# Scores and value products of a local attention in four parts a tile, and a new order of steps on four engines

## What is computed

```python
# per layer i, per batch b:       x: 256 tokens x 128 channels
q, k, v = split(shift_tokens(x) @ Wqkv[i])            # 16 heads of 64
q, k = rotary(l2norm(q) * qs), rotary(l2norm(k) * ks)
# windows of 32 queries, each sees its own 32 keys and the 32 before
sim  = einsum('bhwie,bhwje->bhwij', bq, bk2) * 8      # 32 x 64 scores
attn = softmax(where(mask, -max, sim), -1)
out  = einsum('bhwij,bhwje->bhwie', attn, bv2)        # 32 x 64 values
x = out @ Wo[i] + x
xn = layernorm(shift_tokens(x)) * g + bln
a, gate = split(xn @ W1[i] + b1, 2)
x = a * gelu(gate) @ W2[i] + b2 + x
```

## Time and profile before

| | us |
|---|---|
| median of 3 runs | 3975.99 (3974.95 to 3983.92) |
| the profiled execution | 3987.9 |
| its span, first to last instruction | 3986.1 |
| PE busy | 3633.8 (91%), 64569 matmuls |
| DVE busy | 2734.0 (69%) |
| ACT busy | 2766.0 (69%) |
| POOL busy | 1037.4 (26%) |

### The profile page before, as it was taken

The page is one execution under the profiler, slowest core; times in us unless marked ns, Lnnn a source line. Parts: engine busy times, 40 slices in busy tenths (PEclk is TensorE's granted clock), DMA queues, the critical chain, the costliest instruction groups (busy, mean ns, idle before and its releaser), DMA issues.

```text
span 3986.1 us, 157311 instructions
## 1 busy us (share of the span) xinstructions
PE 3633.8 (91%) x64569; PEld 2525.9 (63%) x64761; DVE 2734.0 (69%) x5376; ACT 2766.0 (69%) x9073; POOL 1037.4 (26%) x857
## 2 busy tenths in 40 slices
PE   6776999999999999999999999999999999999997
PEld 3333666666666666666666666666666666666665
DVE  3334777777777777777777777777777777777774
ACT  3443776776777776777777677777777777777775
POOL 0001232232232233232223223223223223223220
PEclk7556999999999999999999999999999999999998
DMA  1001555445455445455545454545554545544452
GB/s 49 7 7 31 115 115 121 108 106 137 105 119 122 107 111 136 107 121 117 116 111 125 114 125 105 124 106 123 122 117 109 120 112 123 115 114 110 111 121 68
DMA packets 361465, 421.61 MB, mean 106 GB/s; under 512 B 52480, under 2 KB 266000, under 8 KB 360000
## 3 DMA queue, kind: packets, MB, share of 16 engines
q1 hardware_dynamic: 360768, 411.67, 44.8%
HBM read 19.30 MB, written 2.10 MB: 5 GB/s over the span
## 4 chain that ended last, share of the span: by engine, by line
PE 77%; ACT 9%; issue 5%; DVE 0%; SPq 0%; DMA 0%; POOL 0%; DVEq 0%; ACTq 0%
PE ring_ps L1062 18%; PE out_ps L1176 8%; PE ring_ps L1109 7%; PE score_ps L1127 7%; PE out_ps L1204 7%; PE out_ps L1164 7%; ACT probs L659 6%; PE turn_ps L1146 6%; PE turn_ps L1138 4%; PE small_ps L1073 4%; PE turn_ps L1211 2%; PE score_ps L1117 2%; ACT att_t L647 1%; ACT L641 1%; PE out_ps L1194 1%
## 5 line engine op out<-in xcount | busy, mean ns | idle before, releaser
L659 ACT ACTIVATE probs<-score_ps,neg_max,rq 128x64 f32<-128x64 f32 x3072 | 1191.7, 418 | 185.9 <-DVE neg_max L876 184.7
L838 DVE TENSOR_TENSOR prod<-ring_ps,tables 128x512 f32<-128x512 f32 x1536 | 951.4, 681 | 157.3 <-PE ring_ps L1062 146.5
L532 POOL TENSOR_TENSOR ks<-prod 128x1024 f32<-128x1024 f32 x192 | 451.5, 2352 | 2102.8 <-DVE prod L838 2018.6
L1062 PE MATMUL ring_ps<-xs,wqk 128*128 128x256 f32 x3072 | 765.7, 387 | 11.9 <-DVE xs L825 5.1
L614 ACT ACTIVATE square<-ring_ps,biases 128x512 f32<-128x512 f32 x768 | 507.1, 687 | 252.0 <-DVE prod L838 229.7
L659 ACT ACTIVATION_READ_ACCUMULATOR probs<-score_ps,neg_max,rq 128x1 f32 x3072 | 673.6, 219 | 0.0
L1062 PEld LDWEIGHTS ring_ps<-xs,wqk 128*128 128x128 f32 x3072 | 555.5, 191 | 116.3 <-issue 41.1
L647 ACT ACTIVATE att_t<-turn_ps 128x512 f32<-128x512 f32 x384 | 229.3, 597 | 501.0 <-PE turn_ps L1146 501.0
L532 POOL TENSOR_TENSOR qs<-prod 128x1024 f32<-128x1024 f32 x192 | 451.9, 2354 | 243.5 <-DVE prod L838 235.9
L1164 PE MATMUL out_ps<-v,pt 64*32 64x64 f32 x24576 | 349.7, 224 | 88.5 <-issue 87.1
L1109 PE MATMUL ring_ps<-wv,xs 128*128 128x512 f32 x768 | 405.5, 631 | 1.0 <-issue 1.0
(11 more groups left out here) (156 smaller groups left out, 4483.7 us busy)
## 6 DMA issues: line engine op xcount, KB each, us to landing
v<-vs SPq DMA_DIRECT2D x1344, 128.0 KB
qt<-qs SPq DMA_DIRECT2D x768, 128.0 KB
kt<-ks SPq DMA_DIRECT2D x768, 128.0 KB
v<-vs SPq DMA_DIRECT2D x192, 64.0 KB
wqk<-in_L_ffn_Wqkv SPq DMA_DIRECT2D x6, 1024.0 KB, 5.2
wv<-in_L_ffn_Wqkv SPq DMA_DIRECT2D x6, 512.0 KB
wo<-in_L_ffn_Wo SPq DMA_DIRECT2D x6, 512.0 KB
prod<-in_L_attn_x SPq DMA_DIRECT2D x16, 128.0 KB, 2.1
```

The lines of the kernel that those rows point to most:

```text
L532: pool.tensor_tensor(dst, prod_a[p % 2], prod_b[p % 2], ALU.add).then_inc(rot_ready, 1)
L659: last = nc.scalar.activation(probs[i][:, j, e, :], score_ps[e][:, KEYS * j:KEYS * (j + 1)], ACT.Exp, bias=neg_max[:, h:h + 1], scale=rq[p ...
L838: last = V.tensor_tensor((prod_b if a else prod_a)[p % 2][:, f, :] .rearrange("p (u c) -> p u c", u=2), bank[:, :].rearrange("p (u c) -> p ...
L1062: last = mm(bank_of(s, parity)[:, TOKENS * f:TOKENS * (f + 1)], wqk[:, n, 2 * c + f, a, :], xs[:, WINDOW:PADDED], start=True, stop=True)
```

## The change

`S` and `PV` get four parts a tile in place of two: a part is 16 small products (32 matmuls and 32 weight loads in the trace). The semaphores are raised after the last part (`part == 3`), and `PV` waits for the copy of the probabilities in its parts 0 and 2. The four places in the code where PE calls `alone` in the pipeline are gone, which is eight instructions a period. And four of the five orders are new. `SP_ORDER` stays.

```diff
 PE_ORDER = """
-PA0 PB0 S00 S01 PA1 PB1 BI WO PA2 PB2 CEN NK T00 VAR PA3 TK PB3 UP0 S10 S11 UP1 UP2 TU T01 NQ KN0 PV00 DN KN1
-PV01 TQ T10 V0 V1 T11 PV10 O00 PV11 V2 O01 V3 O10 O11
+PA0 S00 PB0 S01 S02 S03 PA1 PB1 BI WO T00 PA2 CEN NK PB2 VAR TK S10 PA3 S11 UP0 PB3 S12 S13 UP1 TU UP2 NQ T01
+PV00 KN0 KN1 PV01 PV02 DN PV03 T10 V0 V1 T11 PV10 PV11 O00 PV12 PV13 O01 V2 V3 O10 TQ O11
 DVE_ORDER = """
-XS RA0 RB0 M0 RA1 RB1 BI XA XB RA2 RB2 CK XG TC00 RB3 RA3 H0 M1 H1 H2 UC TC01 CQ KM0 X KM1 TC10 AT0 TC11 VC1 AT1
-VC3
+XS RA0 RB0 M0 RA1 RB1 BI XA XB TC00 RA2 CK RB2 XG RA3 RB3 H0 M1 H1 H2 UC TC01 KM0 KM1 X AT0 TC10 CQ TC11 VC1 AT1
+VC3
 ACT_ORDER = """
-QA0 QB0 E00 QA1 QB1 E01 E02 SQ QA2 QB2 LN E03 RTK LG G0 QB3 QA3 G1 G2 LE E10 E11 E12 E13 VC0 RTQ OC00 OC01 VC2
-OC10 OC11
+QA0 QB0 E00 E01 QA1 QB1 E02 SQ E03 QA2 LN RTK QB2 LG G0 QA3 QB3 G1 G2 LE E10 E11 E12 E13 VC0 OC00 OC01 VC2 OC10
+RTQ OC11
 POOL_ORDER = """
-AD0 AD1 AD2 RK AD3 TB
+AD0 AD1 RK AD2 AD3 TB
...
                 if kind == "TU":
-                    alone(pe)
...
                 if kind == "KN":
-                    alone(pe)
...
-                    if i == 0 and half == 0:
+                    if i == 0 and part == 0:
                         pe.wait_ge(k_moved, moved(g, 1))
                         pe.wait_ge(q_moved, moved(g, 1))
-                        alone(pe)
-                    for j in range(PAIRS // 2 * half, PAIRS // 2 * (half + 1)):
+                    for j in range(PAIRS // 4 * part, PAIRS // 4 * (part + 1)):
...
                 if kind == "PV":
-                    i, half = s[1], s[2]
-                    pe.wait_ge(t_copied, at(g, 2 * TILES, 2 * i + half + 1))
-                    if half == 0:
+                    i, part = s[1], s[2]
+                    if part % 2 == 0:
+                        pe.wait_ge(t_copied, at(g, 2 * TILES, 2 * i + part // 2 + 1))
+                    if part == 0:
...
-                    alone(pe)
-                    for j in range(PAIRS // 2 * half, PAIRS // 2 * (half + 1)):
+                    for j in range(PAIRS // 4 * part, PAIRS // 4 * (part + 1)):
```

More of the change, by code:

```diff
@@ L1130, in step @@
                                           start=False, stop=True, skip_group_check=True)
-                    if half == 1:
+                    if part == 3:
                         last.then_inc(s_ready, 1)
```

## The result

| | median, us | runs |
|---|---|---|
| before | 3975.47 | 3973.96 to 3983.92 (4) |
| changed | 4073.51 | 4070.21 to 4075.21 (4) |

The ratio is 1.0241, 95% interval 1.0223 to 1.0259: slower by 98 us, where 44 were forecast. The profiled execution has a span of 4071.0 us against 3986.1, 85 more.

What follows compares the result with a forecast made beforehand. PE's own work, its gaps and whoever feeds it were taken to bound the kernel; blocks +65, stalls -35, waits +19, gates and moves 0 gave +49 us, 4025 from the 3976 median, rounded to 4020 us; range 3935 to 4075.

Steps and rivals of the forecast that it cites:

- Blocks: PE's small products: six blocks become ten, four added at 0.17 us each, 0.68 a period, +65 us (31 to 119).
- fast start: PE's small products: a block starts faster than it goes on, so 0.17 us an added block, on the low side.
- Waits: PE's waits at O11 (-0.2 us), PB1 (+0.15) and T10 (+0.3): net +0.25 a period, taken as 0.2, +19 us.
- Moves to other places on POOL, ACT, DVE: RTQ, CQ and E03 moved: each needed 5 us or more later or moving with what it feeds; RK has margin: 0.
- Stalls: PE's instruction packets last longer: -15 us before S, -17 before PV, -3 for slow stretches; sum -35 us (0 to -130).
- The echo: PE after a long stall: a following window at granted clock 0.50, the 1.2 GHz level; 3 us of relief taken.
- Gates: Eight alone instructions a period removed from PE: taken as 0, at most -15 us and as much above 0.
- The K move: RK ahead of AD2 delays AD3, MQ and MK: priced 0, with 2.6 us of margin before S00.
- third rival: K move becomes the bound: S00 waits 0.6 us a period, 58 us more, 4080; chance 0.09.
- fourth rival: Skill's rule on instruction fetching: order does not touch "issue", nothing of the -35 us comes, 4060; chance 0.07.
- the signs: PE's waits and timeline afterwards: "issue" near 5 us before S, 70 before PV; undisturbed period 0.7 to 1 us longer.
- first rival: PE's instruction stalls go: 107.8 us and about 20 of slow clock vanish, kernel faster at 3932; chance 0.24.

Runs made afterwards that it cites:

- experiments 11 and 12: A quarter of ACT's exponentials left out, in the changed kernel (3938.28 us, 0.9913) and in experiment 1's old-order kernel (3932.84 us, 0.9891).
- E01: Not a run: a step of ACT's order, exponentials of tile 0 that T00 on PE waits for.
- E03: Not a run: a step of ACT's order, the last exponentials of tile 0 (four, 1.5 us), which read the banks that S10 writes.
- experiment 2: Changed kernel with T00 back behind NK on PE, TC00 behind RA2 on DVE and QA1 QB1 ahead of E01 on ACT: 4071.83 us, 1.0268.
- f2: Experiment 1's kernel with S of tile 1 spread among TK, PB3 and UP0 as in the changed kernel: 4164.92 us, 1.0483.
- experiments 13, 14: Kernel before with 165 idle semaphore instructions a period on PE, 5331.3 us (1.3451); then the same with 104 fewer in the prologue, 5638.82 us.
- experiment 1: Changed kernel's code (four parts, no gates) with the old orders on all engines, parts side by side in six blocks: 3939.54 us, 0.9938.
- experiment 15: Experiment 1's kernel with eight idle semaphore instructions a period on PE, put between large steps: 3961.0 us, 0.9972.
- experiment 14: The padded kernel with 104 fewer idle semaphore instructions in the prologue, shifting packet ends into the small products: 5638.82 us in one run.
- the shortened changed kernel: Changed kernel with a quarter of ACT's exponentials left out, other engines' work the same: 3938.28 us, 0.9913.
- the shortened old order: Experiment 1's kernel, in the old orders, with a quarter of ACT's exponentials left out: 3932.84 us, 0.9891.
- the padded kernel: Kernel before with 165 idle semaphore instructions a period on PE between large steps, 1536 instructions a period: 5331.3 us, 1.3451.

## Why the prediction was wrong

The kernel got slower, as forecast, but by +98 us for +44, and for a reason that the forecast did not contain. The steps, per period:

- **Blocks, +0.68 forecast.** The mechanism was right and the size a little low: with the loop out of the way PE's own work is 0.85 longer (experiments 11 and 12). The rows show the edges. PE's timeline of the changed kernel at `S00`:

```profile
2936.77 1.03 PE L1062 MATMUL ring_ps<-xs,wqk 128*128 128x256 f32 x4
2937.63 0.59 PE L1115 MATMUL score_ps<-mask_bf,ident_bf 128*128 128x512 bf16 x2
2938.16 0.46 PE L1124 MATMUL score_ps<-kt,qt 64*32 64x64 f32 x32
2938.54 1.13 PE L1062 MATMUL ring_ps<-xs,wqk 128*128 128x256 f32 x4
2939.60 1.17 PE L1124 MATMUL score_ps<-kt,qt 64*32 64x64 f32 x96
```

  `PA0` ahead of the masks takes 0.86 to the next start (2936.77 to 2937.63), `PB0` between `S00` and `S01` 1.06: leaving a block and going into the next cost 0.20 together. The 32 products themselves are quick, 0.38, as the "fast start" supposed. The Trainium skill's rule (page "TensorEngine Tiling (Array Packing)", section "Key Properties", a change of mode drains the array) shows in that 0.20, and as I had weighed it, below its full 0.31 a block.
- **Waits, +0.2 forecast: the step that failed.** "Net +0.25 a period; ... so 0.2." Of the three waits that I had listed, `O11` fell to 46.0 from 66.7 us, as forecast; `T10` waits 15.9 us for DVE (0.2 a period for 0.3); `PB1` has no line of its own in the list. The sum had no wait of PE for ACT's exponentials. `T00` and `T11` wait for them 0.44 and 0.45 us in an undisturbed period, and the loop that they stand in costs 1.5 a period (37.3 - 35.83), 140 us, where I had 19 for all waits. Two things let it in. `T00` behind `WO`, which calls for `E01` earlier, stood in the diff and in no step of mine. And the step "Moves to other places on POOL, ACT, DVE" says "each is needed 5 us or more later, or moves with what it feeds. 0." That fails for `E03`. In the changed kernel its last instruction and `S10`, which overwrites the banks that `E03` reads, are

```profile
2951.07 0.29 ACT L659 ACTIVATION_READ_ACCUMULATOR probs<-score_ps,neg_max,rq 128x1 f32 x1
2951.53 0.59 PE L1115 MATMUL score_ps<-mask_bf,ident_bf 128*128 128x512 bf16 x2
```

  0.17 us apart. `S10` hardly waits there (0.4 us, once in the run), for `T00` waits ahead of it; with `T00` back it does (experiment 2), and with `E03` late it costs +2.2 us a period (f2). I asked of each moved step whether its consumer was near, one at a time, and never added up a cycle. Experiment 2 shows that pricing `T00` alone would not have been enough.
- **Stalls, -0.36 forecast (-35 us).** The mechanism was right (experiments 13, 14), the size too low: what disturbance adds to a period fell by 1.06 us, 102 in all. 49 of it are "issue" before `S` and `PV` (107.8 to 58.4), of which 5 were the wait of `PV10` behind its gate. The echo of the earlier trace rows adds up to 15: in the pipeline without its last two periods, stretches of 3.4 us at granted clock 0.50 fell from 16 to 7, and each gives away up to 1.7 us; I had put 3. The other 38 I can't place. Much of the relief is not the order's: of the 44 us of stalls, 30 are gone in experiment 1 already, whose order is the old one.
- **Gates, 0 forecast.** "No row shows PE's array idle for one" was a misreading: a wait that ends at a gate shows as "issue", and `PV10` had 32 of them. Without the gates the old order gained 25 us. How, stays open (experiment 15).
- **The K move** (third rival) is not there: one wait of 3.4 us in the whole run. The fourth rival falls with experiment 14. Of the signs, "issue" before `S` came as forecast (4.5 for 5), before `PV` lower (53.9 for 70) and far from the first rival's 20; the undisturbed period is longer by 1.95 where 0.7 to 1 was the sign.
- **The sum** with measured terms: (0.48 own work and small waits + 1.47 loop - 1.06) x 96 = 85, the spans' difference. The 0.48 is the 0.6 of experiments 11 and 12 less what the old order gave back there. Without the loop this is (0.48 - 1.06) x 96 = -56: the terms that I had, in their measured sizes, make a faster kernel, and the shortened changed kernel is one (0.9913; the shortened old order has 0.9891, with overlapping intervals, so against the same code the new order without its loop is a wash at best). So the sign of the forecast was luck: the term that was missing (140) is larger than the one that was too small (67). The time lies inside the range, near its upper end, for the same reason.

## What to carry to other kernels

When an order is made anew, follow the whole cycle from one period's step to the same step of the next through every engine, and sum it, instead of asking of each moved step whether its consumer is near; look also at who must have read a buffer before the moved step may write it. To tell whether a loop or an engine's own work sets the period, shorten another engine's work and nothing else: 3.1 us less on ACT gave back 1.5 here and 0.2 in the old order. And where many small instructions stand together, count the instruction stream: a shift of the packets' ends alone made 241 us of stalls among the products of `PV` where there had been none.

## What the runs showed of the hardware

- An idle semaphore instruction on PE is not free. 165 of them between large steps lengthen the undisturbed period from 35.4 to 50.5 us, 0.09 us each. The granted clock is part of that: its mean over the pipeline falls to 0.85 (busy by window, the columns as above), which gives away up to 0.15 x 50.5 = 7.6 us a period. So between 0.05 and 0.09 us are left for an instruction. The waits of that kernel list it as "issue" before the large steps:

```profile
446.00:5297.00 4851.00, 3891.56 (x63117) 2594.93 (x63306) 2617.52 (x4817) 2603.68 (x8514) 990.36 (x790) 0.85 0.36 84
...
PE ring_ps L1067 <- issue: 259.5, 230, 3.9
```

- The instruction queue of the padded kernel moved 577 packets against 516: 61 more for 15708 added instructions, 258 each. Semaphore instructions fill packets like any other.
- An exponential of 64 columns with its sum is two instructions on ACT, 0.193 us each in a row (4.05 / 21), 0.39 in all.
